# Turning the second attention's probabilities with crossbar DMA transposes in place of TensorE transposes

## The reference

```python
h = gelu(x[:, 1:] @ W[:256] + x[:, :1] @ W[256:] + b)          # token projection
u = layernorm(h)                                               # first attention: cosine similarity, no mask
h = h + softmax(u @ u.T / (|u_i| |u_j|)) @ u + u
x2 = layernorm(h)                                              # second attention, with 8 experts of width 128
logits = normalised(x2) @ normalised(sim_matrix) - sigmoid(gates)
m = logits > 0 (the two largest where none is)                 # expert mask per token
q, k, v = sum over experts e of m[:, e] * (x2 @ {q,k,v}_proj[e])
p = softmax(causal(q @ k.T / sqrt(128)))                       # 374 x 374, lower triangle
a = p @ v
h = h + sum over experts e of m*route[:, e] * (a @ o_proj[e])
```

## Time and profile before

| | |
|---|---|
| median of 3 runs | 709.33 us (708.91 to 710.06) |
| span of the profiled execution, first to last instruction | 708.6 us |
| TensorE busy | 703.0 us (99%) |
| TensorE weight loads | 467.6 us (66%) |
| VectorE | 572.1 us (81%) |
| GpSimd | 402.7 us (57%) |
| ScalarE | 373.1 us (53%) |
| DMA, mean over the span | 56 GB/s, 22% of the 16 engines' time |

### The profile page before, as it was taken

The page is one execution under the profiler, slowest core; times in us unless marked ns, Lnnn a source line. Parts: engine busy times, 40 slices in busy tenths (PEclk is TensorE's granted clock), DMA queues, the critical chain, the costliest instruction groups (busy, mean ns, idle before and its releaser), DMA issues.

```text
span 708.6 us, 18356 instructions
## 1 busy us (share of the span) xinstructions
PE 703.0 (99%) x5356; PEld 467.6 (66%) x5356; DVE 572.1 (81%) x1456; ACT 373.1 (53%) x808; POOL 402.7 (57%) x669
## 2 busy tenths in 40 slices
PE   9999999999999999999999999999999999999997
PEld 8888666665757666575756666575766656575655
DVE  5888898887979888787979888787988878786736
ACT  4977373554546364553646355454646356364443
POOL 7642326756466566746566575646556674653434
PEclk9999999999999999999999999999999999999999
DMA  9681230303021030302111030303113020301121
GB/s 242 150 190 48 63 78 6 96 2 86 14 67 33 12 88 0 93 7 73 27 47 52 7 93 0 88 12 67 33 18 81 0 93 7 77 26 53 15 75 30
DMA packets 57975, 39.87 MB, mean 56 GB/s; under 512 B 29928, under 2 KB 53720, under 8 KB 57816
## 3 DMA queue, kind: packets, MB, share of 16 engines
q1 hardware_dynamic: 57552, 39.16, 21.8%
q10 hardware_dynamic: 392, 0.32, 0.2%
HBM read 30.45 MB, written 9.01 MB: 56 GB/s over the span
## 4 chain that ended last, share of the span: by engine, by line
PE 97%; DMA 1%; issue 1%; POOL 0%; ACTq 0%; POOLq 0%; DVE 0%; ACT 0%; DVEq 0%
PE bank L1752 77%; PE bank L1815 7%; PE bank L1669 5%; PE bank L1726 3%; PE bank L1658 2%; PE bank L1886 2%; PE bank L1801 1%; PE bank L1674 1%; DMA region_b<-in_x_dram 1%; PE bank L1837 0%; PE bank L1826 0%; PE bank L1829 0%; POOL region_c L699 0%; POOL region_c L692 0%; PE bank L1706 0%
## 5 line engine op out<-in xcount | busy, mean ns | idle before, releaser
L1752 PE MATMUL bank<-xm,w_qkv 128*128 128x374 f16 x2304 | 415.7, 322 | 0.0
L1752 PEld LDWEIGHTS bank<-xm,w_qkv 128*128 128x128 f16 x2304 | 221.4, 98 | 140.9
L961 ACT ACTIVATE region_c<-bank,out_w 128x256 f32<-128x256 f32 x180 | 85.0, 472 | 170.6 <-PE bank L1752 169.5
L1341 DVE TENSOR_TENSOR xm<-xT,mask_all 128x1496 f16<-128x1496 f16 x128 | 154.6, 1230 | 0.1
L1752 PE MATMUL bank<-w_o,aoT 128*128 128x512 f16 x540 | 143.3, 379 | 0.0
L1245 DVE SCALAR_TENSOR_TENSOR h<-bank,out_w,h 128x256 f32 (+1 forms) x180 | 86.0, 478 | 54.7 <-ACT region_c L961 49.1
L692 POOL TENSOR_TENSOR region_c<-region_c 128x512 f32<-128x512 f32 x46 | 78.5, 1706 | 27.8 <-ACT region_c L961 22.8
L729 POOL TENSOR_TENSOR exp_hl<-exp,exp_hl 128x128 f16<-128x128 f32 (+2 forms) x48 | 34.2, 714 | 83.2 <-ACT exp_hl L903 83.2
L1752 PEld LDWEIGHTS bank<-w_o,aoT 128*128 128x128 f16 x540 | 50.0, 98 | 39.6
L699 POOL TENSOR_TENSOR region_c<-region_c 128x256 f32<-128x256 f32 x46 | 46.9, 1019 | 8.1 <-POOL region_c L692 7.9
L1815 PE MATMUL bank<-xhl,exp_hl 128*128 128x257 f16 (+1 forms) x432 | 50.3, 272 | 0.0
(11 more groups left out here) (205 smaller groups left out, 1059.3 us busy)
## 6 DMA issues: line engine op xcount, KB each, us to landing
mask_all<-d_mask SPq DMA_DIRECT2D x32, 384.0 KB, 4.2
h<-in_x_dram SPq DMA_DIRECT2D x16, 256.0 KB, 4.9
out_dram<-h SPq DMA_DIRECT2D x31, 128.0 KB
rnorm_row<-d_rnorm SPq DMA_DIRECT2D x16, 192.0 KB, 3.9
d_v<-xinT SPq DMA_DIRECT2D x14, 192.0 KB, 4.4
xinT<-d_v SPq DMA_DIRECT2D x56, 48.0 KB, 2.3
h<-in_x_dram SPq DMA_DIRECT2D x15, 112.0 KB, 5.6
out_dram<-h SPq DMA_DIRECT2D x15, 112.0 KB
```

Source lines behind the costliest of these rows:

```text
L961: a.activation(prod[:, prod_buf(n, t), q, :], pair_bank(n, p)[:, C:2 * C], ACT.Copy, scale=weights_out(n)[:, t, 2 * q + 1:2 * q + 2]).then ...
L1341: v.tensor_tensor(xm[:, e, :, 0:T], xT[1][:, :, :, 0:T].rearrange("p a c t -> p (a c) t"), mask_all[:, e, 0:T].unsqueeze(1).broadcast_to([ ...
L1752: last = t_.matmul(dst, left[lp], right[rp], start=(starts and k == 0), stop=(stops and k == 2), skip_group_check=True)
```

## The change

For batches 0 to 13, the 12 TensorE transposes of a step, the copy on VectorE and the copy on ScalarE are gone. SyncE issues six crossbar DMA transposes in their place, one for each query tile and half, straight from `exp2_hl` to `pT` in SBUF. Each of the three for the high half waits for its tile's `s_exp2_hi`; the three for the low half wait for `s_exp2_lo`. `probs_v` waits for all six (`s_pT_moved`). Six transposes are called at the head of SyncE's step, before the norms. Batches 14 and 15 keep the TensorE way. `pT` gets another layout, with a fixed distance between the blocks of one query tile, so that one DMA can write them: 7 block places for each half in place of 6. To keep every place defined, batches 14 and 15 turn 7 blocks for each half and copy 896 columns in place of 768. The wait for `s_h2_ready` that stood ahead of the second group of transposes now stands ahead of `M(8)`. Two small head tiles (`read_row`, `read_hl`) now lie in `exp2`, and the counters that only mark passed waits are one semaphore.

```diff
-    PT_OFF = [sum(TP - P * jj for jj in range(j)) for j in range(NT)]
+    PT_OFF = [NT * P * j for j in range(NT)]
+    PT_BLOCKS = NT + (NT - 1) * (NT - 1)
...
-        pT = sb("pT", [P, 2, PW], F16)
+        pT = sb("pT", [P, 2, PT_BLOCKS * P], F16)
...
+            def probs_around(n):
+
+                def move(p, i):
+                    blocks = pT[:, p, :].rearrange("p (k q) -> p k q", q=P)
+                    sp.dma_start_transpose(blocks[:, i:i + (NT - 1) * i + 1:NT - 1, :],
+                                           exp2_hl[:, p, S_OFF[i]:S_OFF[i] + (i + 1) * P]).then_inc(s_pT_moved, 16)
+
+                for i in range(NT):
+                    sp.wait_ge(s_exp2_hi, NT * n + i + 1).then_inc(s_passed, 1)
+                    if i == 0 and later(n):
+                        sp.wait_ge(s_pv_done, n).then_inc(s_passed, 1)
+                    move(0, i)
+                sp.wait_ge(s_exp2_lo, n + 1).then_inc(s_passed, 1)
+                for i in range(NT):
+                    move(1, i)
...
             def step(i, g, f, m, n):
+                if n is not None and by_trip(n):
+                    probs_around(n)
...
             def low_probs(n):
-                if later(n):
-                    pool.wait_ge(s_pT_lo_turned, n).then_inc(s_pool_passed, 1)
+                if final(n):
+                    pool.wait_ge(s_pT_lo_turned, n - 1 - LAST_TRIP).then_inc(s_passed, 1)
+                elif later(n):
+                    pool.wait_ge(s_pT_moved, 32 * NT * n).then_inc(s_passed, 1)
...
                     residual(f)
-                    turned_probs_low(n)
                     if g1 is not None:
                         norm_stats(0, g1)
...
             def probs_v(n):
-                pe.wait_ge(s_pT_hi, n + 1)
-                pe.wait_ge(s_pT_lo, n + 1)
                 if by_trip(n):
+                    pe.wait_ge(s_pT_moved, 32 * NT * (n + 1))
                     pe.wait_ge(s_v_tok_ready, 2 * (n + 1))
...
-                    M(6)
-                    turn_probs_low(n)
-                    M(7)
-                    turn_probs_high(n, f)
+                    M(6, 7)
+                    pe.wait_ge(s_h2_ready, NT * (f + 1))
                     M(8, 9)
                     probs_v(n)
                     M(10)
                     pe.wait_ge(s_hi2, f + 1)
-                    pe.wait_ge(s_pT_lo, n + 1)
                     turn_rows(1, f, 0, turn[0], s_turned2_hi)
```

More of the change, by code:

```diff
@@ L292, in audio_tower_kernel @@
         s_pT_lo = sem("pT_lo")
+        s_pT_moved = sem("pT_moved")
         s_pv_done = sem("pv_done")
@@ L514, in last_stores @@
                     cols = slice(half * C // 2, (half + 1) * C // 2)
[L515 removed]
+                    sp.wait_ge(s_last_ready, 2 + half).then_inc(s_passed, 1)
                     sp.dma_start(out[n, 2 * P:2 * P + SPLIT, cols], h[0:SPLIT, n, 2, cols]).then_inc(s_stored, 16)
             def route_around():
[L520 removed]
+                sp.wait_ge(s_weigh_pool, 6 * B).then_inc(s_passed, 1)
                 sp.dma_start(d_route.rearrange("(t e p) -> p t e", t=NT - 1, e=E), route_w[:, B - 1, 1:NT, :],
                              allow_slow_non_contiguous=True).then_inc(s_route_stored, 16)
[L523 to L525 removed]
+                sp.wait_ge(s_route_stored, 16).then_inc(s_passed, 1)
+                sp.wait_ge(s_lo1, B).then_inc(s_passed, 1)
+                sp.wait_ge(s_lo2, B).then_inc(s_passed, 1)
                 sp.dma_start(route_row.rearrange("p t e q -> p (t e q)"),
@@ L895, in exp_scores @@
                 if i == 0:
+                    if final(n):
+                        act.wait_ge(s_pT_lo_turned, n - 1 - LAST_TRIP)
+                    elif later(n):
+                        act.wait_ge(s_pT_moved, 32 * NT * n)
                     if later(n):
-                        act.wait_ge(s_pT_lo_turned, n)
                         act.wait_ge(s_sum2_s, n)
@@ L941, in turned_probs @@
             def turned_probs(n):
-                act.wait_ge(s_pT_hi_turned, n + 1)
-                if later(n):
-                    act.wait_ge(s_pv_done, n)
-                a.activation(pT[:, 0, :], as16(turn[1], PW), ACT.Copy).then_inc(s_pT_hi, 1)
+                act.wait_ge(s_pT_hi_turned, n - LAST_TRIP)
+                act.wait_ge(s_pv_done, n)
+                a.activation(pT[:, 0, :], as16(turn[1], PT_BLOCKS * P), ACT.Copy).then_inc(s_pT_hi, 1)
             def step(i, g1, f, m, n):
@@ L1446, in turned_probs_low @@
             def turned_probs_low(n):
-                dve.wait_ge(s_pT_lo_turned, n + 1)
-                if final(n):
-                    dve.wait_ge(s_pv_done, n)
-                v.tensor_copy(pT[:, 1, :], as16(turn[0], PW)).then_inc(s_pT_lo, 1)
+                dve.wait_ge(s_pT_lo_turned, n - LAST_TRIP)
+                dve.wait_ge(s_pv_done, n)
+                v.tensor_copy(pT[:, 1, :], as16(turn[0], PT_BLOCKS * P)).then_inc(s_pT_lo, 1)
             def step(i, g1, f, m, n):
@@ L1872, in turn_probs_low, with turn_probs_high, turn_probs @@
                     pe.wait_ge(s_scores_out, NT * (n + 1))
-                elif not by_trip(n):
+                else:
                     pe.wait_ge(s_v_tok_ready, 2 * (LAST_TRIP + 1) + n - LAST_TRIP)
                 turn_probs_half(1, turn[0], s_pT_lo_turned)
-            def turn_probs_high(n, f):
-                if f is not None:
-                    pe.wait_ge(s_h2_ready, NT * (f + 1))
+            def turn_probs_high(n):
                 turn_probs_half(0, turn[1], s_pT_hi_turned)
             def turn_probs_half(p, dst, done):
-                for i in range(NT):
-                    for j in range(i + 1):
-                        at = PT_OFF[j] + (i - j) * P
-                        last = t_.transpose(as16(dst, PW)[:, at:at + P],
-                                            exp2_hl[:, p, S_OFF[i] + j * P:S_OFF[i] + (j + 1) * P], ident16[:, :])
+                used = [(PT_OFF[j] + (i - j) * P, S_OFF[i] + j * P) for i in range(NT) for j in range(i + 1)]
+                unused = [(at, 0) for at in range(0, PT_BLOCKS * P, P) if at not in [u[0] for u in used]]
+                for at, of in used + unused:
+                    last = t_.transpose(as16(dst, PT_BLOCKS * P)[:, at:at + P], exp2_hl[:, p, of:of + P], ident16[:, :])
                 last.then_inc(done, 1)
-            def turn_probs(n, f=None):
+            def turn_probs(n):
                 turn_probs_low(n)
-                turn_probs_high(n, f)
+                turn_probs_high(n)
             def probs_v(n):
-                pe.wait_ge(s_pT_hi, n + 1)
-                pe.wait_ge(s_pT_lo, n + 1)
                 if by_trip(n):
+                    pe.wait_ge(s_pT_moved, 32 * NT * (n + 1))
                     pe.wait_ge(s_v_tok_ready, 2 * (n + 1))
                 else:
+                    pe.wait_ge(s_pT_hi, n - LAST_TRIP)
+                    pe.wait_ge(s_pT_lo, n - LAST_TRIP)
                     pe.wait_ge(s_v_tok_ready, 2 * (LAST_TRIP + 1) + n - LAST_TRIP)
```

139 lines of the change are left out of this document (68 added, 71 removed).

## The result

The changed kernel took 722.97 us (median of 4 runs, 722.35 to 724.32) against 709.22 us of the kernel before in 4 runs next to it (708.91 to 710.06): ratio 1.0195, with a 95% interval of 1.018 to 1.0209. That is 13.8 us slower. The profiled execution has a span of 720.6 us, 12.0 us above. The forecast was 709.5 us with the transposes in time. What came is, by its time and its mark in the profile, the rival "late by 0.1 to 2.3 us".

A forecast was written before the change was run, and what follows sets the result against it. Taken as bound: a chain on other engines to each step's first turning of normalised rows. 14 steps x 0 - 0.1 + 0.33 = +0.2 us on a 708.6 us span, plus 0.7 around it: 709.5 us; range 707.5 to 750 us.

The forecast's parts named there:

- late by 0.1 to 2.3 us: Rival at `p @ v`: the last DMA transpose lands that much too late, 711 to 742 us; chance 0.31.
- in time and nothing won: Likeliest case: transposes land before `p @ v` needs them and removed TensorE work gains nothing, 708.8 to 711 us; chance 0.44.
- The wait ahead of the turning: TensorE's wait before first turning the normalised rows, for ScalarE's cast: to grow from 0.19 to 0.86 us, step length unchanged.
- the saved TensorE time comes out: Rival: with the chain 0.67 us earlier, the removed TensorE work wins 9.4 us, 700 us; chance 0.08.
- Issue: 0.30 to 0.36 us: SyncE's issue time per transpose, from store, norms (0.30 to 0.36 us) and values' loads (0.59 us); three 1.0 to 1.8 us.
- 4.7 us from the low half's readiness: Time for the low half's three transposes, from readiness at 309.67 to the latest harmless `p @ v` start, 314.41.
- The landing, 2.8 us: Last transpose's 96 KB, taken between 2.3 us for 48 KB and 3.9 us for 192 KB: in time by 0.7 to 1.2 us.
- the transposes don't overlap: Rival at `p @ v`: each low-half transpose lands before the next moves, 2.2 us late, +31 us, 740 us; chance 0.31.
- the transposes are slow in themselves: Rival at `p @ v`: six full landings queue up or cost like `d_route`, +75 to +98 us, 785 to 807 us; chance 0.17.
- the chain get shorter: Whether removed VectorE and ScalarE copies shorten the other engines' chain to the turning: both worth 0; 0.1 us taken overall.
- The third rival: Saved TensorE time comes out if VectorE or GpSimd is quicker between 306.17 and 314.31: 9.4 us won, 700 us; chance 0.08.
- The end, +0.33 us: Batches 14 and 15 turn 14 blocks in place of 12: 0.11 + 0.11 us for batch 15, 0.11 us for batch 14.

The follow-up runs named there:

- kernel 1: The changed kernel with the six DMA transposes of every step left out and nothing in their place (pT zero): 709.83 us, ratio 1.0003 to the kernel before.
- kernel 2: The changed kernel with the low half's three transposes as one DMA of six blocks: 704.07 us, ratio 0.9918 to the kernel before.
- kernel 6: The kernel without any transposes (kernel 1) plus one already fulfilled ScalarE wait with a register-multiplied target: 704.76 us, ratio 0.993 to the kernel before.
- kernel 8: The changed kernel with six plain DMA copies of the same blocks, unturned, in place of the transposes: 704.19 us, ratio 0.9922 to the kernel before.
- kernel 7: Kernel 2 with ScalarE waiting for `s_pv_done`, target unmultiplied, in place of the DMAs' counter: 709.45 us, ratio 0.9996 to the kernel before.

## Why the prediction went as it did

The measured 722.97 us lies within the stated 707.5 to 750 us, but the forecast was 709.5 us, on the likeliest case (0.44, in time and nothing won), and that case did not come. The range holds because it was stretched over the rivals, and the time fell to one (0.31) whose stated mechanism was another than the one found. What the working had right is the bound; what it had wrong is the issue on SyncE.

- **What bounds the kernel, and that the removal buys nothing:** right. The wait ahead of the turning grew to 0.86 us in kernel 1, the number worked out, and the time was 709.83 us. The rival that the saved TensorE time comes out (700 us) is refuted in that form.
- **"Issue: 0.30 to 0.36 us ... 0.59 us ... Three issues are 1.0 to 1.8 us, the last one starts at 310.4 to 310.9":** this step failed. A transpose takes 1.12 to 1.26 us to issue, and the low half's three, from the first start to the last end, 3.7 us. On the clock of the working, which is 4.13 us behind that of the changed kernel in this step (`neg_max` at 304.85 and 308.98), the last starts at 316.93 - 4.13 = 312.80 in place of 310.9 at the latest. The working bounded the landing from both sides, but the issue of an operation that the trace didn't hold only by near rows of other kinds of DMA.
- **"So the last three transposes have 4.7 us from the low half's readiness":** the same step's second half. It took SyncE to be free when the low half is ready. The low half was ready at 313.95 - 4.13 = 309.82 (0.15 us later than taken, by ScalarE's register instruction), and SyncE took it up at 310.35, after the high half's issues. Six issues had to be laid on the queue, not three.
- **The landing, 2.8 us:** mis-sized to the safe side, 2.36 us. With the measured start the same sum closes: 312.80 + 2.36 + 0.12 to TensorE's start = 315.28 against the deadline of 314.41, 0.87 us late where the trace has 0.89.
- **"The six issues and their waits delay nothing, even if each took 1.5 us":** right for SyncE's other work, the norms. It was asked only what stands behind the transposes, and not what they do to each other. The text named the trigger itself ("a transpose that takes over 1 us to issue on SyncE"), and that is what came.
- **The rival "the transposes don't overlap":** its time (711 to 742 us) and its mark in the profile (a DMA in front of `pT,v_tok`, no wait ahead of the turning) came. Its mechanism did not: the transfers do overlap; the issues do not. Three landings of 2.3 us one after the other would have ended at 313.95 + 6.9 = 320.85, and the last landed at 319.29; and each start, 1.2 us behind the one before, lies ahead of the landing of that one.
- **The rival "the transposes are slow in themselves" (0.17):** did not come. Each landed 2.2 to 2.4 us after its issue's start in this step, and six blocks in one instruction in 2.7 us (kernel 2), and all six of the step had landed 8.9 us after the first one's start (310.43 to 319.29). So neither full landings one behind the other came, nor blocks turned one after another, for which the prediction had 15.7 us (306.0 to 321.7).
- **"Does it [the chain get shorter]?":** incomplete. The text looked only for removed work. The chain was 0.48 us shorter, by an added instruction on an engine with time to spare. The third rival's condition ("VectorE or GpSimd quicker between 306.17 and 314.31") was thus met. In the changed kernel it bought nothing; kernels 2, 6 and 8 lie 4.8 to 5.5 us under the kernel before, more than half of the 9.4 us; with the removal, but not the shorter chain, kernels 1 and 7 win nothing.
- **The end, +0.33 us:** the copies of 896 columns took 917 ns, 0.11 us more than the earlier trace rows, as taken. The total of +0.3 us agrees with the medians of kernel 1 (+0.28 us), which the interval can't tell from nothing; its profiled span, 708.4 us, is 0.2 us under the earlier trace rows. So the size of this term stays open.
- **"The 0.7 us around it":** a slip. It set a median beside the span of another, slower execution; span and time of one execution lie 1.67 to 1.80 us apart. The forecast change of +0.2 us does not hang on it.

In sum: the step that failed is the issue, taken as 0.30 to 0.59 us for each transpose and measured as 1.12 to 1.26 us, on a queue that was taken as free at 309.67 and was not. It made the step 0.87 to 0.89 us longer, some 12.3 us in 14 steps; the removal was worth 0.

## What to carry to other kernels

- When compute is turned into DMAs, sum the issue times on the issuing queue as well as the landing, all of them from the first to the last, and take the issue of an unseen kind of DMA as open. Here a crossbar transpose cost 1.2 us per instruction for one to six blocks, so merging the blocks into fewer instructions took the lateness away. That alone brings the kernel back to 709.45 us (kernel 7), the time of before; 704.07 us (kernel 2) needs the shorter chain as well.
- Work that is removed from the busiest engine is worth nothing while a chain on other engines sets its next wait, and something as soon as that chain gets shorter (0 and 2.3 us here, kernels 1 and 6); look at the start-to-start distances, not the busy share.
- Where two engines' instructions start close together and slow each other (0.13 us apart here), a small edit ahead of them can turn the order. Compare the durations of unchanged instructions in both traces before a gain or loss is put down to the edit.

## What the runs showed of the hardware

- A DMA transpose (float16, SBUF to SBUF) took 1.12 to 1.27 us on SyncE's queue for one, two or three blocks of 128 x 128 in 83 of the changed kernel's 84 issues (the other took 1.76 us), and 1.21 to 1.22 us for six blocks (kernel 2); a plain DMA of the same shape (kernel 8) 0.49 to 0.69 us.
- It landed 2.2 to 2.4 us after the start of its issue in the step shown, while the next was being issued; with six blocks, 2.7 us (kernel 2).
- A wait on ScalarE whose target is a product with the loop's register in place of a wait without a multiplication cost 0.15 us between two dependent instructions (0.33 to 0.48 us), though its condition was long met.
- A float16 product on VectorE (1,496 columns, two tiles read) and a subtraction on GpSimd (256 columns) slow each other by order of start: 0.93 and 1.44 us when VectorE starts 0.03 us ahead, 1.41 and 0.75 us when GpSimd starts 0.13 us ahead.
